# The loads of a pair of heads go behind its products with V, in a fused cross-attention and feed-forward kernel

## What is computed

```
x = x + xattn(layernorm(x), ctx)            # no causal mask; a key mask and a bias per head
    q, k, v = xn @ Wq, ctx @ Wk, ctx @ Wv   # 512 -> 32 * 128 each
    p = softmax(q k^T / sqrt(128) + bias, masked keys left out)
    out = (p v) @ Wo                        # 32 * 128 -> 512
x = x + ffn(layernorm(x))
    base = xn @ base_W^T + base_b
    w = the 8 largest of softmax(xn @ router_W^T + router_b), summed by expert
    base + 2 * ((xn @ A^T) * w) @ B^T       # 8 experts of rank 16
```

## Time and profile before

| | |
|---|---|
| median of 3 runs | 790.44 us (788.65 to 790.91) |
| the profiled execution, its own time | 791.96 us |
| its span, first to last instruction | 790.1 us |
| PE busy | 780.8 us (99%), 6360 matmuls |
| PE weight loads busy | 652.0 us (83%), 6360 |
| DVE busy | 521.5 us (66%) |
| ACT busy | 399.9 us (51%) |
| POOL busy | 185.3 us (23%) |
| TensorE's granted clock, mean | 0.998 of full speed |
| DMA | 118.40 MB, mean 150 GB/s |

### The profile page before, as it was taken

The page is one execution under the profiler, slowest core; times in us unless marked ns, Lnnn a source line. Parts: engine busy times, 40 slices in busy tenths (PEclk is TensorE's granted clock), DMA queues, the critical chain, the costliest instruction groups (busy, mean ns, idle before and its releaser), DMA issues.

```text
span 790.1 us, 16795 instructions
## 1 busy us (share of the span) xinstructions
PE 780.8 (99%) x6360; PEld 652.0 (83%) x6360; DVE 521.5 (66%) x951; ACT 399.9 (51%) x1138; POOL 185.3 (23%) x203
## 2 busy tenths in 40 slices
PE   8999999999999999989999999999999999999998
PEld 7888888888888888878888888888888888887886
DVE  6883626267677665577666776676667676657974
ACT  5663525246556555573665456535654466435520
POOL 0225041024333434232222122212211221010200
PEclk9999999999999999999999999999999999999999
DMA  6536773245544547583564355534563355342002
GB/s 226 199 121 220 225 243 138 109 139 159 190 160 159 169 154 215 171 250 111 164 182 135 110 157 161 163 110 130 162 177 115 112 160 176 109 118 83 2 6 103
DMA packets 108078, 118.40 MB, mean 150 GB/s; under 512 B 44239, under 2 KB 77007, under 8 KB 107998
## 3 DMA queue, kind: packets, MB, share of 16 engines
q1 hardware_dynamic: 107998, 117.31, 47.7%
HBM read 81.64 MB, written 35.65 MB: 148 GB/s over the span
## 4 chain that ended last, share of the span: by engine, by line
PE 93%; DMA 2%; DVE 2%; SPq 1%; issue 1%; ACT 0%
PE pY L1393 42%; PE pP L1393 39%; PE pY L1552 4%; PE pO L1577 2%; PE pT_ L1577 2%; PE pS L1562 1%; DMA wv_raw<-in_L_xattn_Wv 1%; PE pO L1393 1%; PE pT_ L1562 1%; DMA v<-v_hbm 1%; DMA k_hbm<-stage 1%; SPq L425 1%; DVE st L980 1%; PE pS L1577 1%; DVE y L1129 0%
## 5 line engine op out<-in xcount | busy, mean ns | idle before, releaser
L1129 DVE TENSOR_TENSOR y<-y,pY 128x512 f32<-128x512 f32 x124 | 84.6, 682 | 24.6 <-PE pY L1393 24.2
L1393 PE MATMUL pY<-wo_hi,oT_hi 128*128 128x512 f32 x248 | 97.4, 393 | 1.2 <-issue 1.2
L1393 PE MATMUL pY<-wo_lo,oT_hi 128*128 128x512 f32 x248 | 97.2, 392 | 0.0
L1393 PE MATMUL pY<-wo_hi,oT_lo 128*128 128x512 f32 x248 | 97.2, 392 | 0.0
L910 DVE TENSOR_TENSOR wk_lo<-wk_raw,wk_hi 128x256 fp32r<-128x256 f32 x96 | 46.7, 487 | 62.2 <-ACT wk_hi L651 61.3
L759 ACT ACTIVATE pr<-pr,mx 128x64 f32<-128x64 f32 x256 | 86.2, 344 | 2.8 <-DVE mx L1146 2.8
L651 ACT CAST wk_hi<-twk 128x256 fp32r<-128x256 f32 x128 | 50.7, 409 | 64.5 <-PE pP L1393 53.6
L1393 PE MATMUL pP<-xo_hi,wk_hi 128*128 128x512 f32 x196 | 78.1, 399 | 0.0
L1393 PE MATMUL pP<-xo_hi,wk_lo 128*128 128x512 f32 x196 | 76.6, 391 | 0.0
L1393 PE MATMUL pP<-xo_lo,wk_hi 128*128 128x512 f32 x196 | 76.4, 390 | 0.0
L584 POOL TENSOR_TENSOR bias<-bias,madd 128x512 f32<-128x512 f32 x32 | 41.5, 1308 | 148.2 <-DMA bias<-in_fside_Bx32xSxS 148.2
(11 more groups left out here) (282 smaller groups left out, 1896.6 us busy)
## 6 DMA issues: line engine op xcount, KB each, us to landing
v_hbm<-stage SPq DMA_DIRECT2D x64, 256.0 KB, 2.3
k_hbm<-stage SPq DMA_DIRECT2D x64, 256.0 KB, 3.6
k<-k_hbm SPq DMA_DIRECT2D x16, 1024.0 KB, 5.1
v<-v_hbm SPq DMA_DIRECT2D x16, 1024.0 KB, 7.0
wk_raw<-in_L_xattn_Wk SPq DMA_DIRECT2D x16, 512.0 KB, 4.4
wo_raw<-in_L_xattn_Wo SPq DMA_DIRECT2D x16, 512.0 KB, 3.7
bias<-in_fside_Bx32xSxS SPq DMA_DIRECT2D x128, 64.0 KB, 3.6
wk_raw<-in_L_xattn_Wq SPq DMA_DIRECT2D x16, 512.0 KB, 4.7
```

The source lines that it names most:

```text
L1129: nc.vector.tensor_tensor(y[:, t, :], y[:, t, :], src[:, :], ALU.add).then_inc(y_added, 1)
L1393: mm = nc.tensor.matmul(bank_, a, b, start=first and n == 0, stop=last and n == len(terms) - 1, skip_group_check=read_between)
```

## The change

- **v of pair 0** gets a place of its own, `v0`, in memory that the parts of ctx have left. `load_v(0)` no longer waits for the last blocks of K to be stored; these waits stand ahead of `load_v(1)`. It is issued ahead of the last store of block QA and of a load of weights.
- **SP's loop**: the wait for `o_full` moves up, right behind the load of Wo. Behind it come the biases, k, the next weights and v.
- **The feed-forward's small inputs** move: base_b, router_b and the expert map to pair 1, A and the router's weights to pair 2, base_W to pair 3, B to pair 4, into memory that `v0` and the parts of ctx have left, so that they wait for nothing more. The selector on VectorE moves from pair 0 to pair 3.
- **The two alignments** of TensorE's stream are gone.
- **Warm-up**: 14 transpositions of 128 columns become 12 of these and 26 of 32 columns by 32 partitions.
- **VectorE** makes c21 of block QB ahead of the low part of Wo of pair 0.
- **Tail**: ScalarE copies the outputs of pair 14 ahead of four exponentials; blocks 4 and 5 of the feed-forward weights stand later, on all three engines.

The core of the diff:

```diff
+        v0 = at("v0", R0 + 16384, [P, NT, 2 * DH])
...
-                sp.dma_start(v[:, :, :], v_hbm[i // 2, :, :, i % 2 * 2 * DH:(i % 2 + 1) * 2 * DH]
+                sp.dma_start((v if i else v0)[:, :, :], v_hbm[i // 2, :, :, i % 2 * 2 * DH:(i % 2 + 1) * 2 * DH]
...
             store(QA, 1, c12_made)
+            sp.wait_ge(prod, DONE[QA, 4])
+            load_v(0)
+            store(QA, 2, c21_made)
             load_wk(QA - 9)
-            store(QA, 2, c21_made)
-            sp.wait_ge(prod, DONE[QA, 4])
-            (loads of base_b, router_b and the expert map)
-            for i in range(4):
-                sp.wait_ge(put[0][i], 16 * (QA // 2 + 1))
-            load_v(0)
             for i in range(NP - 1):
                 sp.wait_ge(wo_l, i + 1)
                 load_wo(i + 1)
+                sp.wait_ge(o_full, 4 * (i + 1))
                 if i + 2 < NP:
-                    sp.wait_ge(s_full, 2 * i + 4)
-                    load_k(i + 2)
                     for s in range(2):
                         sp.wait_ge(s_read, 2 * i + 3 + s)
                         load_bias(2 * i + 4 + s)
+                    sp.wait_ge(s_full, 2 * i + 4)
+                    load_k(i + 2)
                 if i + 24 < NSET:
                     load_wk(i + 24)
-                sp.wait_ge(o_full, 4 * (i + 1))
+                if i == 0:
+                    for n in range(4):
+                        sp.wait_ge(put[0][n], 16 * (QA // 2 + 1))
                 load_v(i + 1)
...
ScalarE, tail:
-            exp(h + 2, 0)
             o_high(h, 0)
             o_high(h, 1)
             o_high(h + 1, 0)
             o_high(h + 1, 1)
+            exp(h + 2, 0)
             exp(h + 2, 1)
...
-            split_ffn(4)
             turned_p(h + 2)
             turned_p(h + 3)
-            split_ffn(5)
+            split_ffn(4)
             o_high(h + 2, 0)
             o_high(h + 2, 1)
             o_high(h + 3, 0)
             o_high(h + 3, 1)
+            split_ffn(5)
             split_ffn(6)
...
VectorE:
+            make_c21(QB)
             lower_wo(0)
-            make_c21(QB)
...
TensorE:
-            warm_up(14)
+            warm_up(12)
+            warm_up(26, 32)
...
-            nc.tensor.addr_align(256, offset=142)
...
-                if i % 3 == 2:
-                    nc.tensor.addr_align(256, offset=18)
...
             for t in range(4, NT):
                 times_wo(i, t)
-                if t == 5:
-                    ffn_weights(4)
             turn_p(h + 2)
             turn_p(h + 3)
-            ffn_weights(5)
+            ffn_weights(4)
             times_v(h + 2)
             times_v(h + 3)
+            ffn_weights(5)
             ffn_weights(6)
```

More of the change, by code:

```diff
@@ L145, in xattn_ffn @@
                for n, part in enumerate(("hi", "lo"))] for i in range(2)]
+        v0 = at("v0", R0 + 16384, [P, NT, 2 * DH])
+        a_raw = at("a_raw", R0 + 16384, [P, D])
+        r_raw = at("r_raw", R0 + 18432, [NR, D])
+        b_raw = at("b_raw", R0 + 20480, [P, DC, ER])
+        bw_raw = at("bw_raw", R0 + 24576, [P, DC, D])
         r0 = R0 + 49152
@@ L172, in xattn_ffn @@
         fw = [at("fw_hi_", R1 + 32768, [P, DC, D], F32R), at("fw_lo_", R1 + 40960, [P, DC, D], F32R)]
-        bw_raw = at("bw_raw", R1 + 49152, [P, DC, D])
         R2 = 114688
@@ L503, in _ @@
             store(QA, 1, c12_made)
+            sp.wait_ge(prod, DONE[QA, 4])
+            load_v(0)
+            store(QA, 2, c21_made)
             load_wk(QA - 9)
-            store(QA, 2, c21_made)
-            sp.wait_ge(prod, DONE[QA, 4])
-            sp.dma_start(bb[:, :], base_b.partition_broadcast(P)).then_inc(ld_small, 16)
-            sp.dma_start(rb[:, :], router_b.partition_broadcast(P)).then_inc(ld_small, 16)
-            sp.dma_start(mapi[:, :], emap.partition_broadcast(P)).then_inc(ld_small, 16)
-            for i in range(4):
-                sp.wait_ge(put[0][i], 16 * (QA // 2 + 1))
-            load_v(0)
             for i in range(NP - 1):
@@ L521, in _ @@
                         load_bias(2 * i + 4 + s)
+                    sp.wait_ge(s_full, 2 * i + 4)
+                    load_k(i + 2)
                 if i + 24 < NSET:
                     load_wk(i + 24)
-                sp.wait_ge(o_full, 4 * (i + 1))
+                if i == 0:
+                    for n in range(4):
+                        sp.wait_ge(put[0][n], 16 * (QA // 2 + 1))
                 load_v(i + 1)
-                if i == NP - 4:
-                    sp.wait_ge(w_lo[5], NSET - 1)
-                    sp.wait_ge(tw_made, 4 * (NSET - 1))
+                if i == 1:
+                    sp.dma_start(bb[:, :], base_b.partition_broadcast(P)).then_inc(ld_small, 16)
+                    sp.dma_start(rb[:, :], router_b.partition_broadcast(P)).then_inc(ld_small, 16)
+                    sp.dma_start(mapi[:, :], emap.partition_broadcast(P)).then_inc(ld_small, 16)
+                if i == 2:
                     sp.dma_start(a_raw[:, :], a_d).then_inc(ld_a, 16)
                     sp.dma_start(r_raw[:, :], router_W).then_inc(ld_a, 16)
-                if i == NP - 3:
-                    sp.wait_ge(prod, len(ORDER))
+                if i == 3:
                     sp.dma_start(bw_raw[:, :, :], bw_d).then_inc(ld_ffn, 16)
+                if i == 4:
                     for o in range(DC):
@@ L1247, in _ @@
                 add_tile(i, 7)
-                if i == 0:
+                if i == 3:
                     dve.wait_ge(ld_small, 48)
@@ L1464, in turn_pair, with warm_up @@
                     turn(xn[:, (m + 1) % NX, :], second_turn(j))
-            def warm_up(count):
+            def warm_up(count, n=P):
                 for _ in range(count):
-                    nc.tensor.transpose(pY[1][:, 0:P], ident[:, :], ident[:, :])
+                    nc.tensor.transpose(pY[1][0:n, 0:n], ident[0:n, 0:n], ident[0:n, 0:n])
             pe.wait_ge(made, 1)
@@ L1577, in times_v @@
                             mm = nc.tensor.matmul(pO_of[s][i][64 * d:64 * d + 64, t * S:(t + 1) * S],
-                                                  v[rows, t, s * DH + 64 * d:s * DH + 64 * d + 64],
+                                                  (v if h >= 2 else v0)[rows, t, s * DH + 64 * d:s * DH + 64 * d + 64],
                                                   pT[s][rows, t, :], start=True, stop=True)
@@ L1659, in _ @@
                 times_v(h + 1)
-                for p in (1, 2) if i else (2,):
-                    times(n, p)
-                if i % 3 == 2:
-                    nc.tensor.addr_align(256, offset=18)
-                for p in (6, 7):
+                for p in (1, 2, 6, 7) if i else (2, 6, 7):
                     times(n, p)
```

3 lines of the change are left out of this document (removed).

## The result

| | before | changed |
|---|---|---|
| median of 14 runs each, one chip | 790.33 us (788.65 to 793.37) | 788.72 us (787.74 to 790.36) |
| ratio of the two | | 0.9979, interval 0.9970 to 0.9989 |
| profiled execution, its span | 791.96 us, 790.1 us | 787.74 us, 786.0 us |
| granted clock over the span | 0.998 | 1.00 |

The forecast was 786.3 us, a move of -4.1 us. The two profiled executions differ by 4.2 us, almost the sum forecast. But the one of before lies 1.6 us above its median, and the one after is the fastest of its 14.

What follows compares the result with a forecast made beforehand. TensorE bounds the kernel, busy 780.8 of 790.1 us. Terms -1.6 -0.35 -0.3 +0 -0.64 -0.44 -0.8 +0 = -4.1 us, taken from the median 790.44, give 786.3 us; range 784.0 to 789.9.

Steps and rivals of the forecast that it cites:

- (e): Tail: copies ahead of exponentials and moved feed-forward blocks close holes of 0.64 and 0.54 us, for -0.64 and -0.44 us.
- (a): Loads of pair 0: earlier v ends a 0.35 us wait, quiet queues take 1.6 us off the code pause.
- (b): Pair 0: making c21 of QB ahead of the low part of Wo ends the 0.33 us wait for q, -0.3 us.
- (c): Loop's loads behind o_full: all still land in time, tightest slack on the path v's 9.4 us; cost 0.
- (d): Alignments removed: five blocks pause instead of three pairs, 1.2 us against 1.3; change 0, bounds -0.7 and +1.4.
- (f): Tail: clock falls to 0.51 for 3.4 us, priced at 1.7 us; half taken as gain, -0.8 us.
- (g): Start: 26 small transpositions at 32 ns add 0.56 us net, hidden in a 0.61 us wait; cost 0, bounds 0 and 3.0.
- Rival B: Pause moves with the code blocks, five pay, quiet queue does not shorten it, clock still falls: 789.3 us, chance 0.15.
- Rival E: In the loop v, last in the burst behind o_full, lands late and TensorE waits every pair: 800 us, chance 0.05.

Runs made afterwards that it cites:

- its twin: The kernel before, run again unchanged for a second profile: 789.81 us, ratio 0.9993 between the two identical kernels.
- tail only: Kernel before with only the tail changed (output copies ahead of the exponentials, feed-forward blocks 4 and 5 later): 788.93 us, ratio 0.9981.
- loads only: Kernel before with only the new places and new order of transfers: 791.17 us, ratio 1.0007.
- all but the transfers: Changed kernel with SP's list, the places in memory and the loads of the kernel before: 788.30 us, ratio 0.9973.

## Why the prediction was wrong, step by step

Where the 4.1 us went, by the names of the prediction:

- **(e) tail**, forecast -1.08 us: right. 20.11 to 18.96 us at full clock is -1.15, and tail only showed it by itself. The holes were in every trace of before.
- **(a) and (b) pair 0**, forecast -2.25: measured -1.5 (26.79 in the mean of before, its twin and tail only, 25.29 in that of three traces of the changed kernel). What was forecast to go went: v was there, the packet came at once (345.26 in place of 348.56), no pause. The size was read from the worst of three traces: in its twin the pause was absent, in tail only 0.89 us. Part of the gain is lost again to what is late next, the 0.41 us at 352.30; the text had looked for it at the copy of the turned weights. That the moved v takes the pause away is not borne out: loads only kept a pause of 1.14 us, all but the transfers had none, and the traces point at edit (b), which delays the load of Wo. Of the wait for q, the kernel with only the transfers lost it without the reordering: wo_lo takes 1.22 us there, with no GpSimd operation beside it, and 1.76 in the earlier trace rows; the reordering was one of two sufficient edits.
- **(c) the loads behind o_full**, forecast "Cost 0": this step failed. I had asked only whether TensorE or GpSimd would get the data in time, and they do: no wait of TensorE for k or v in any trace with these loads. I hadn't asked whom GpSimd's mask addition runs beside when it runs later. Price: 1.2 us (788.26 against 787.04 on one chip); in the traces, 0.8 to 1.5 us of waits of weight loads, which the biases back where they were take away.
- **(d) the alignments**, forecast 0 for the sum: this gained a little. The text took three pairs at 0.42 us each for the kernel before, 1.3 us; the pairs have 0.42, 0.34 and 0.34 over, 1.1 us. Over 13 x 25.73, pairs 1 to 13 had 0.78 to 1.19 us before (tail only with it), 1.04 to 1.55 after, and 0.13 to 0.44 with the biases back. With the waits of the weight loads for y subtracted, which are 0 before, 0.1 to 0.3 us are left after: on the mean some 0.7 us of pauses are gone. With the old warm-up and the alignments back 0.9 us are left, pauses of 0.13, 0.15 and 0.32 us among them, and the kernel is 1.0 us slower (789.25 against 788.26), though more meetings of the kind of (c) are part of that. So this part paid back much of (c).
- **(f) the clock**, forecast -0.8 "I take half": a quarter of executions fall, at about 1.3 us each (29 runs of before on one chip: the median of the 7 fallen is 791.68, of the other 22 it is 790.37). That is -0.3 us of a mean, and less of a median. The three times shown before could not tell half from a quarter.
- **(g) start**, forecast 0: right in the first profile only. The first product stands at 7.55 there, but at 7.75 and 8.74 in the other two of the changed kernel, and later than 7.6 was among the signs that the forecast is wrong. With the old warm-up it stands at 7.49 to 7.58 in four traces, and at 8.00 in one, behind a wait of 1.18 us for ctx. Pair 0 starts at 343.31 to 343.62 in the three traces with the old warm-up and the old transfers, at 343.63 with only the warm-up new of these two, at 343.97 and 344.68 with only the transfers new, and at 343.68 to 344.57 with both new. In the kernel with nothing new but the warm-up, the same matmul (pP<-b_hi,co_lo) stands at 19.03 that before stands at 18.12. All of it arises in the first 20 us, where no transfer was changed. About +0.6 us, and the runs don't show which edit it comes from.

In sum, from traces: +0.6 - 1.5 + 0.3 - 1.15 and -0.3 for the clock, -2.05 us; the three ratios of the changed kernel say -1.7, -3.1 and -2.0. Two steps failed. One is "Cost 0" in (c), a wait that the forecast had at nothing. The larger one stands behind the sum, the sentence "I move it by the same": a difference worked out against one execution, of which the text itself knew that it lay 1.5 us above the median, was carried over whole. The excess of 1.5 us was made of the very losses being removed: the fall of the clock (1.6 us in this trace, 21.72 against 20.11 for pair 14) and the longest of the pauses. Rival B named 789.3, within 0.6 us of the measured median, for a wrong reason (five pauses), so that is luck; no trace of the changed kernel has a pause over 0.05 us. Rival E, a late v, did not show anywhere.

What stays open: what delays a code packet by up to 3 us, since the load of Wo is only the nearest suspect, and what makes the first 20 us longer.

## What to carry to other kernels

A profile that lies above the median of the runs holds losses which most executions don't have: price the change by it, then take the excess off the gain before it is moved to the median. When a transfer is moved, follow not only its deadline but also the operation that it releases, and see what runs beside that on another engine, as the mask addition did beside VectorE's low part. When an edit changes the order of one engine's list, ask which transfers wait for what has moved: making c21 first also delayed the load of Wo. Code alignments hold only for the exact number of instructions ahead of them: one edit far ahead can turn 22 fillers into 230.

## What the runs showed of the hardware

- A small transposition of 32 columns in a row of them takes 40 ns, a filler of an alignment about 66 ns, an estimate (15.2 us for 230 by count).
- TensorE's code block can run 2.3 to 2.45 us after its packet has started, and the packet can start anywhere from 0.4 us before the first matmul of the block before it to 2.9 us after (345.09 against 345.50, 348.56 against 345.68).
- An addition of 128x512 on GpSimd (1.30 us) holds a VectorE operation of 0.42 us with two inputs in the SBUF until it is over: the operation ended 0.28 us behind the addition, after 1.49 us.
- A run of short operations with a hole of 0.64 us was followed by 3.4 us at half clock in one profile of the kernel before, and the same run by none in the second. A wait of 2.86 us was followed by such a fall in the one profile that has it; 8 of that kernel's 12 executions had a mean clock of 1.00.
